# A softmax-like loop partly on GpSimd, two earlier weight streams and a finer side job in an eight-core transformer kernel

## The reference

```python
xn = _layernorm(x, axis=-1)
# attention-like branch
qkv = _rms(xn) @ w_qkv.T
q, k, v = jnp.split(qkv, 3, axis=-1)
q = _rms(q); k = _rms(k)
w = jnp.exp(k)
kv_cum = jnp.cumsum(w * v, axis=1)
w_cum = jnp.cumsum(w, axis=1)
y = jax.nn.sigmoid(q) * (kv_cum / (w_cum + 1e-06))
u, g = jnp.split(y @ w_swiglu.T, 2, axis=-1)          # 2 x 8192
attn = xn + u * jax.nn.silu(g) @ w_out.T
# second branch, fwht: Walsh-Hadamard transform of the last axis
t = fwht(xn * SU_ug) / SCALE
t = silu(t @ W_gate.T * (Wscale_ug[INTER:] * SCALE)) * (t @ W_up.T * (Wscale_ug[:INTER] * SCALE))
ffn = (fwht(t * SU_dp) / SCALE) @ W_down.T * (Wscale_dp * SCALE)
return x + attn + ffn
```

## Time and profile before

| | us |
|---|---|
| Three runs: median | 12506.38 |
| Three runs: lowest, highest | 11569.87, 12691.81 |
| The profiled execution, its own time | 11569.87 |
| Its span, slowest core | 11568.3 |
| Busy, TensorE matmul | 8165.5 (71%) |
| Busy, VectorE | 4189.6 (36%) |
| Busy, ScalarE | 1977.1 (17%) |
| Busy, GpSimd (DMA issues, all but four small memsets) | 437.3 (4%) |

### The profile page before, as it was taken

The page is one execution under the profiler, slowest core; times in us unless marked ns, Lnnn a source line. Parts: engine busy times, 40 slices in busy tenths (PEclk is TensorE's granted clock), DMA queues, the critical chain, the costliest instruction groups (busy, mean ns, idle before and its releaser), DMA issues. The chain is left out here.

```text
span 11568.3 us, 100573 instructions; the slowest of 8 cores (11511.4 to 11568.3 us)
## 1 busy us (share of the span) xinstructions
PE 8165.5 (71%) x35072; PEld 3480.9 (30%) x35072; DVE 4189.6 (36%) x4832; ACT 1977.1 (17%) x2180; POOL 437.3 (4%) x796
## 2 busy tenths in 40 slices
PE   3555552895225466377787788888888869797979
PEld 1222220342002122133333333333333324343434
DVE  4445551565650361377677751111111110000111
ACT  1111111000011231211111111222222223230000
POOL 0000000000000000000000000000000000000000
PEclk8777776997568788699899999999999979898989
DMA  4111101211110011233433332222222235554343
GB/s 73 44 44 44 44 30 65 96 73 29 22 38 33 33 45 59 70 122 109 137 117 116 132 110 79 96 81 75 81 74 81 75 118 171 179 172 155 130 160 119
DMA packets 289699, 1021.78 MB, mean 88 GB/s; under 512 B 32691, under 2 KB 147379, under 8 KB 241587
## 3 DMA queue, kind: packets, MB, share of 16 engines
q1 hardware_dynamic: 209270, 772.00, 19.7%
q0 software_dynamic: 79936, 243.34, 7.8%
HBM read 855.81 MB, written 201.35 MB: 91 GB/s over the span
## 5 line engine op out<-in xcount | busy, mean ns | idle before, releaser
L108 PE MATMUL ps_u<-A_big,wt 128*128 128x512 bf16 x8192 | 2011.3, 402 | 886.0 <-ACT wt L108 760.3
L108 PE MATMUL ps_o<-A_big,wt 128*128 128x512 bf16 x8192 | 1776.9, 380 | 298.8 <-ACT wt L108 163.6
L108 PE MATMUL ps_g<-A_big,wt 128*128 128x512 bf16 x8192 | 1851.7, 379 | 0.0
L108 PE MATMUL ps_m<-A_big 128*128 128x512 bf16 x6144 | 1357.3, 385 | 274.1 <-DMA kslabA<-wf_sp 227.5
L108 PEld LDWEIGHTS ps_u<-A_big,wt 128*128 128x128 bf16 x8192 | 829.5, 102 | 2007.8 <-issue 1164.6
L108 PEld LDWEIGHTS ps_o<-A_big,wt 128*128 128x128 bf16 x8192 | 803.2, 98 | 1274.6 <-issue 313.6
L108 PEld LDWEIGHTS ps_g<-A_big,wt 128*128 128x128 bf16 x8192 | 801.2, 98 | 966.9
L108 PE MATMUL ps_m<-A_big,wt 128*128 128x512 bf16 x3072 | 790.4, 419 | 350.8 <-ACT wt L108 279.6
L108 PEld LDWEIGHTS ps_m<-A_big 128*128 128x128 bf16 x6144 | 606.8, 99 | 1037.8 <-issue 332.7
L108 DVE TENSOR_TENSOR midb<-usb,sgf 128x512 bf16<-128x512 bf16 x512 | 354.4, 692 | 1455.7 <-ACT sgf L108 1403.7
L108 ACT CAST wt<-ldb 128x2048 bf16<-128x2048 f32 (+1 forms) x352 | 586.2, 1665 | 459.0 <-DMA ldb<-wswT 236.3
(11 more groups left out here) (110 smaller groups left out, 4681.2 us busy)
## 6 DMA issues: line engine op xcount, KB each, us to landing
ldb<-wswT SPq DMA_DIRECT2D x128, 1024.0 KB, 6.2
ldb<-wugT SPq DMA_DIRECT2D x128, 1024.0 KB, 5.7
wdb<-wdownT SPq DMA_DIRECT2D x16, 4096.0 KB
ldbA<-woutT SPq DMA_DIRECT2D x128, 512.0 KB, 4.4
ldbB<-woutT SPq DMA_DIRECT2D x128, 512.0 KB, 4.7
wt<-wdh_sp SPq DMA_DIRECT2D x32, 2048.0 KB, 10.1
ldb<-wqkvT SPq DMA_DIRECT2D x96, 512.0 KB, 4.6
psw_sp<-midb POOLq DMA_DIRECT2D x256, 128.0 KB, 2.0
```

The source lines that it names most:

```text
L108: r = getattr(h, meth)(*args, **kw)
```

## The change

Four edits. First, in the exp loop of foreign K the multiply into `wtmp` is issued on GpSimd; the sum stays on VectorE, with `redc` of two columns used in turn; the masked accumulate becomes a multiply into `redt` and an add into `carryW`, both on GpSimd. GpSimd's instructions get a semaphore of their own (PO) and, like those of VectorE and ScalarE, a wait for all earlier ones of their engine. The store of `kslab` waits for ScalarE alone. Second, the first two V blocks are streamed before `sig_rows` and the own exp loop, not after. Third, the first two Q blocks are streamed before the last two `v_chain`s. Fourth, `what_gen` yields after each single instruction, and `next(side_gen)` is called three times a tile: once between `usb` and `midb`, twice after `midb`.

```diff
--- before.py
+++ after.py
@@ -48,10 +48,10 @@
     def __init__(self, nc):
         self.nc = nc
         self.sems = {}
         self.streams = None
 
-    AUTO = {"vector": "DV", "scalar": "AC"}
+    AUTO = {"vector": "DV", "scalar": "AC", "gpsimd": "PO"}
 
     def q(self, eng, meth, *args, w=(), i=None, **kw):
         if eng in self.AUTO and meth not in ("_wait_only_", "dma_start"):
...
@@ -334,7 +334,8 @@
             bcs = S("bcs", [128, 2 * TTK], F32)
             t1f = S("t1f", [128, TTK], F32)
             wtmp = S("wtmp", [128, TTK], F32)
-            redc = S("redc", [128, 1], F32)
+            redt = S("redt", [128, 2], F32)
+            redc = S("redc", [128, 2], F32)
             ps_m = (P("ps_m0", [128, TTK], F32), P("ps_m1", [128, TTK], F32))
             ps_s = (P("ps_s0", [1, TTK], F32), P("ps_s1", [1, TTK], F32))
             ps_sq = (P("ps_sq0", [1, TTK], F32), P("ps_sq1", [1, TTK], F32))
@@ -429,9 +430,10 @@
                     xc = xbf[:, c * TTK:(c + 1) * TTK]
                     wv = []
                     if c == 0:
+                        wv = [("PO", kb.cnt["PO"])]
                         if it >= 2:
-                            wv = [("PE", bigpe[it - 2]),
-                                  (f"SX{par}", xqsp[it - 2])]
+                            wv += [("PE", bigpe[it - 2]),
+                                   (f"SX{par}", xqsp[it - 2])]
                     kb.q("vector", "tensor_mul", t1f[:, :], xc, bcs[:, 0:TTK])
                     dv = kb.q("vector", "tensor_sub",
                               xqf[:, c * TTK:(c + 1) * TTK], t1f[:, :],
@@ -505,23 +507,30 @@
                 sigbcdv[prev] = kb.q("vector", "tensor_copy", t1f[:, :],
                                      ps_b1[:, :], w=[("PE", pe)], i=("DV", 1))
                 ac_p = None
+                po_mac = {}
                 dv = None
                 for j in range(KCH):
                     ks = kslab[:, j * TTK:(j + 1) * TTK]
+                    rj = redc[:, j % 2:j % 2 + 1]
                     wv = [("AC", ac_p)] if ac_p else []
-                    kb.q("vector", "tensor_mul", wtmp[:, :], ks, t1f[:, :],
-                         w=wv)
-                    d2 = kb.q("vector", "engine_nop", i=("DV", 1))
+                    wv.append(("DV", sigbcdv[prev]))
+                    po = kb.q("gpsimd", "tensor_mul", wtmp[:, :], ks,
+                              t1f[:, :], w=wv)
                     ac_p = kb.q("scalar", "activation", ks, wtmp[:, :], AF.Exp,
-                                w=[("DV", d2)], i=("AC", 1))
-                    kb.q("vector", "reduce_sum", redc[:, :], ks, axis=AX.X,
-                         w=[("AC", ac_p)])
-                    dv = kb.q("vector", "scalar_tensor_tensor",
-                              carryW[:, j:j + 1], redc[:, :],
-                              cmsk[:, f3:f3 + 1], carryW[:, j:j + 1],
-                              ALU.mult, ALU.add, i=("DV", 1))
+                                w=[("PO", po)], i=("AC", 1))
+                    wv2 = [("AC", ac_p)]
+                    if j >= 2:
+                        wv2.append(("PO", po_mac[j - 2]))
+                    dv = kb.q("vector", "reduce_sum", rj, ks, axis=AX.X,
+                              w=wv2, i=("DV", 1))
+                    tj = redt[:, j % 2:j % 2 + 1]
+                    kb.q("gpsimd", "tensor_mul", tj, rj,
+                         cmsk[:, f3:f3 + 1], w=[("DV", dv)])
+                    po_mac[j] = kb.q("gpsimd", "tensor_add",
+                                     carryW[:, j:j + 1], carryW[:, j:j + 1],
+                                     tj)
                 wsp[prev] = kb.dma("gpsimd", wf_sp[f3, tt, :, :], kslab[:, :],
-                                   sem="SPI", w=[("DV", dv), ("AC", ac_p)])
+                                   sem="SPI", w=[("AC", ac_p)])
                 bigpe[prev] = kb.cnt["PE"]
 
             emit_cast(0)
@@ -801,6 +810,9 @@
                 evac[pp] = [("DV", d1), ("AC", a2)]
             mmdone[par] = kb.cnt["PE"]
         kb.q("vector", "_wait_only_", w=[("PE", kb.cnt["PE"])])
+        vpar = {}
+        vpar[0] = stream_oc(32 + 0, 0)
+        vpar[1] = stream_oc(32 + 1, 1)
         for tt in range(NT):
             sig_rows(ps_st[tt], tt, bca[:, 0:T], ps_b1)
         ac_p = None
@@ -811,10 +823,6 @@
             ac_p = kb.q("scalar", "activation", kwr_row(j), scf[:, 0:T], AF.Exp,
                         w=[("DV", dv)], i=("AC", 1))
             wexp_ac[j] = ac_p
-
-        vpar = {}
-        vpar[0] = stream_oc(32 + 0, 0)
-        vpar[1] = stream_oc(32 + 1, 1)
 
         def v_chain(j):
             kb.q("vector", "tensor_mul", wvt[:, :], kwr_row(j),
@@ -847,14 +855,17 @@
             mmdone[par] = kb.cnt["PE"]
             if j + 2 < KCH:
                 vpar[j + 2] = stream_oc(32 + j + 2, j + 2)
+            if j == KCH - 1:
+                qpar0 = stream_oc(0, 0)
+                qpar1 = stream_oc(1, 1)
             if j >= 1:
                 v_chain(j - 1)
         dv = v_chain(KCH - 1)
 
         qsp = {}
         qpar = {}
-        qpar[0] = stream_oc(0, 0)
-        qpar[1] = stream_oc(1, 1)
+        qpar[0] = qpar0
+        qpar[1] = qpar1
         for j in range(KCH):
             par = qpar[j]
             for tt in range(NT):
@@ -1037,6 +1048,8 @@
                         ev_u[pp] = kb.q("vector", "tensor_copy", usb[:, S0:S1],
                                         ps_u[pp][:, :], w=[("PE", pe_u)],
                                         i=("DV", 1))
+                    if side_gen is not None:
+                        next(side_gen, None)
                     key = (p, tt)
                     wv = [("AC", ev_g[pp]), ("DV", ev_u[pp])]
                     if key in spq:
@@ -1106,7 +1120,9 @@
                             "p (b w) -> p b w", w=width)
                         kb.q("vector", "tensor_sub", sp_v, a_v, b_v, w=wv)
                         wv = ()
+                        yield
                         kb.q("vector", "tensor_add", a_v, a_v, b_v)
+                        yield
                         dv = kb.q("vector", "tensor_copy", b_v, sp_v,
                                   i=("DV", 1))
                         yield
```

More of the change, by code:

```diff
@@ L50, in __init__ @@
         self.sems = {}
-        self.cnt = {n: 0 for n in ("PH", "LD", "LW0", "LW1", "LQ", "LP0", "LP1", "SPI", "SQ0", "SQ1", "SM0", "SM1", "SO0", "SO1", "LC", "LC1", "SX0", "SX1", "LQ1", "PE", "DV", "AC")}
+        self.cnt = {n: 0 for n in ("PH", "LD", "LW0", "LW1", "LQ", "LP0", "LP1", "SPI", "SQ0", "SQ1", "SM0", "SM1", "SO0", "SO1", "LC", "LC1", "SX0", "SX1", "LQ1", "PO", "PE", "DV", "AC")}
         self.streams = None
-    AUTO = {"vector": "DV", "scalar": "AC"}
+    AUTO = {"vector": "DV", "scalar": "AC", "gpsimd": "PO"}
     def q(self, eng, meth, *args, w=(), i=None, **kw):
@@ L172, in _build @@
     for sname in ("PH", "LD", "LW0", "LW1", "LQ", "LP0", "LP1", "SPI", "SQ0",
-                  "SQ1", "SM0", "SM1", "SO0", "SO1", "LC", "LC1", "SX0", "SX1", "LQ1",
+                  "SQ1", "SM0", "SM1", "SO0", "SO1", "LC", "LC1", "SX0", "SX1", "LQ1", "PO",
                   "PE", "DV", "AC"):
```

## The result

| us | before | after |
|---|---|---|
| Median of 14 executions | 12107.06 | 12451.89 |
| Lowest to highest | 11561.34 to 12717.74 | 11786.43 to 12888.67 |
| The lowest two | 11561.34, 11563.09 | 11786.43, 11789.38 |

Compared like with like, the ratio after to before is 1.0193, with a 95% interval of 1.0163 to 1.0223: slower by 1.9%, at the edge of the 2% that counts as a difference here. The lowest times differ by 225 us. The forecast was 11826, or +256 us on an execution of 11570. The median of all fourteen, 12451.89, lies outside the range of 11620 to 12060.

What follows compares the result with a forecast made beforehand. No engine was taken as full throughout: foreign K was a chain of waits, the pair phase bound by VectorE, then TensorE after the side job. Sum: 11570 + 191 - 4 + 69 = 11826 us, range 11620 to 12060.

Steps and rivals of the forecast that it cites:

- the forecast one: Whole kernel: GpSimd chain in foreign K plus ten tiles behind the side job, 11826 us; chance 0.60.
- forecast +191: Foreign K's exp loop: a 3.93 us step through GpSimd, ScalarE and VectorE, +15.9 us a loop, twelve times.
- X: GpSimd's 128x512 multiply in foreign K's exp loop: taken as 1.2 us, bounds 0.69 to 1.38, far above 3.34.
- h: Hop from VectorE's sum to GpSimd's small multiply in the exp loop: taken as 0.4 us, high end 0.61.
- steps that overlap: Rival, exp loop: GpSimd begins the next multiply during the sum; step 2.20 us, -120 us, kernel 11515 us; chance 0.04.
- forecast -4: V's and Q's weights streamed earlier: about 2 us gained by each; together between a loss and a gain of 12.
- slip of the Ln: ScalarE's Ln of the last-but-one V chain starts about 7 us later, behind Q's casts and loads.
- forecast +69: Side job in single steps, pair phase: +77 us for ten tiles less 8 for shorter idle; high end +96.
- lost slot: Side job: chunks of 12.33 tiles, not 13; last copy at tile 197, not 207; ten tiles after it, +77 us.
- the -8: VectorE under the side job: 186.7 pairs of usb and midb at 1.59 us less 176 at 1.73.
- check of a chunk: Side job before: 12 x 6.12 + 11 x 1.73 + 29.15 = 121.6 us, matching sixteen loads 121.6 apart.
- relieves TensorE: Rival, pair phase: TensorE's 81.6 us of waits for usb go and no tile is lost; -82, 11675 us; chance 0.08.

Runs made afterwards that it cites:

- e5: Edit 1 on the kernel before, with GpSimd's next multiply issued ahead of the two small instructions and wtmp in two halves: foreign K 165.6 us earlier, span 164 us shorter.
- e6: Kernel before, nothing on GpSimd, VectorE's next multiply issued ahead of the sum, wtmp in two halves: foreign K 174.6 us earlier, cores on average 164 us less.
- e3: Edits 2 and 3 alone on the kernel before: 11503.8 to 11570.2 us over eight cores, a mean of 3 us less on die 0.
- e2: Edit 4 alone on the kernel before: pair phase 2340.9 us, lowest time 11627.43 us, +57.7 us.
- e2b: Edit 4 alone on the kernel before, run again for a profile: pair phase 2336.9 us against 2282.8.
- e4: Edit 4 on the kernel before, with two more empty calls behind each store (39 calls, 13 tiles a chunk): pair phase 29.6 us shorter, span 25.
- e1: Edit 1 alone on the kernel before: foreign K 159.5 us longer, lowest time 11737.62 us against 11569.76.
- e10: Kernel before with the next pair's weight loads issued ahead of this pair's tiles: pair phase 17 us shorter, span 6.5.
- e12: Kernel before with VectorE's multiply one chunk ahead, the side job in three parts and weight loads first: lowest 11155.35 us against 11561.88, a factor of 0.965.

## Why the prediction came out as it did

**The case was right, the median was not.** Of the cases, the forecast one happened: a chain through GpSimd, and ten tiles behind the side job. What failed is the base of the sum, 11570, with the sentence "so the forecast is for an execution like it". The range was laid round the lowest of three executions, which was 7.5% under their median, while fourteen executions of the same kernel before spread from 11561.34 to 12717.74. The range took in the price of every edit and left out this larger spread of the metric itself. On the basis it was made for, the error is 31 us (+225 against +256); on the median it is 626. The median of the three, 12506.38, would have given 12762, again 311 off: three executions don't fix a median here.

**Edit 1, forecast +191, measured +157.** 157 / 12 is 13.1 us a loop, not 15.9. The step is 3.73 us, not 3.93 (a row with two engines is a hop, from the end of the one's instruction to the start of the other's):

| term, us | forecast | after |
|---|---|---|
| multiply X | 1.2 | 1.16 |
| GpSimd to ScalarE | 0.2 | 0.15 |
| exp | 0.63 | 0.63 |
| ScalarE to VectorE | 0.17 | 0.23 |
| sum | 0.69 | 0.69 |
| h, VectorE to GpSimd | 0.4 | 0.20 |
| two small instructions | 0.44 | 0.38 |
| their two gaps | 0.20 | 0.29 |

X was well placed, a little under 1.2. The Trainium skill (GPSIMD Engine Reference, 3.1 Elementwise) had led to an estimate of 1.12; the measured 1157 ns lies between it and the value taken. The term that was mis-sized is h. It was put half-way between a hop of 0.17 and a store's delay of 0.61 us behind VectorE, and an arithmetic instruction starts three times sooner than the store, 0.20 us. At fifteen steps and twelve loops 0.2 us make 36 us, as much as the whole error of 34; the other terms cancel.

The cause given was the queue's order, and e5 and e6 show it. The rival "steps that overlap" had been put at a step of 2.20 us and 36.3 us a loop, which the order of the queue ruled out; once e5 changes that order the step is 1.97 and the gain 166 us, more than the 120 it was given. The prediction saw that multiply j+1 stood behind a wait for sum j, but priced it only as a loss against before. It did not ask whether before had the same fault. It had: VectorE's queue, too, held multiply j+1 behind sum j, at 2.89 us a step, where e6 needs 1.91 for the same instructions without the nop.

**Edits 2 and 3, forecast -4, measured about -3 (e3).** Too small to be told from nothing. The slip of the Ln, put at about 7 us, is 8.6 (4445.33 to 4453.95), and V is as long as before. Q is 7.5 us longer in after, and 2 us in e3. Of the 7.5, 3.1 us lie between the last `qtmp` and the first `psw_sp` store (169.4 us against 166.3), where e2, e2b and e4 have 170.0 to 170.5: that is edit 4, whose first side step stands in front of the first `midb`. The other 4.4 us can't be told from the differences between cores: from the first to the last `qtmp` the cores 0 to 3 take 428.7 to 438.1 us in after, but 426.6 to 440.4 in e1, which has none of edits 2 to 4.

**Edit 4, forecast +69, measured +50 (die 0; +54 to +58 in e2b and e2).** The lost slot is right: the last copy falls on tile 197 and not 207, and on core 2 78.4 us more lie behind the side job (381.2 to 459.6), forecast 77. The gap in front of `midb` shrank to 0.10, as written. The term that was mis-sized is the -8: the side job itself became 20 us shorter on core 2 (1929.7 to 1909.7, from its first load to its last store). In before, every fourth chunk takes 102.7 to 104.4 us on core 2 from its first subtract to its last copy, the others 92.3 to 92.7, since VectorE waits in it for TensorE (5.1 us before `usb` and 3.7 before `midb` in the fourth). In after only two of the sixteen are so long, 104.3 and 103.1. In e10, whose weights are loaded earlier, none is (92.3 to 93.1 on core 1), so the long ones come from weights that are late. The prediction had no such term. Its check of a chunk, 121.6 us, came out by luck: the gap of 29.15 us that it read the earlier trace rows is the longest of the fifteen on that core, whose mean is 26.7, and the longer chunks made up the difference. The spacing of the loads on core 2 went from (6716.0 - 4903.9) / 15 = 120.8 to (6865.0 - 5060.7) / 15 = 120.3. The rival "relieves TensorE" is partly true, since e4 gains 25 to 30 us without losing the slot; it was given 82.

**What the prediction left unasked.** It named the gap's load and the 441.2 us of waits for weights behind it, and took both as fixed. 129.8 of the 441.2 are the phase's first wait, ahead of any side job, and e12 has it too (128.3 on core 1). The others and the waits for `usb` were the largest thing in the phase, 256 us, but behind two locks, of which neither alone gives more than 40.

## What to carry to other kernels

Where in-order engines pass work to one another, look first at what stands in front of the next step in each queue, and move that; here, moving the work to a free engine added a hop and left the wait where it was (+157 us, against -166 with the same engines in another order). An empty slot in a hand-paced side job may be the cover of a stall or the place of the last tiles: count the slots before and after. When the removal of one wait gives little, read the waits again for what took its place before giving the idea up: here two locks on the same work paid only together (40 and 17 us alone, 249 both). And where executions of one kernel spread more than the change is worth, say which execution a forecast is for, or give its range the spread.

## What was not expected of the hardware

A 128x1 operation on GpSimd took 0.19 us with VectorE idle or at a one-input sum, but 0.37 to 0.40 in nearly all cases beside a VectorE operation with two inputs. The timeline of core 5 of e5, at the end of a loop:

```profile
674.31 0.97 DVE L108 TENSOR_TENSOR sqbf<-xbfB 128x512 bf16<-128x512 bf16 x2
674.41 0.37 POOL L108 TENSOR_TENSOR redt<-redc,cmsk 128x1 f32<-128x1 f32 x1 [1.24 <-DVE redc L108]
...
674.93 0.40 POOL L108 TENSOR_TENSOR carryW<-carryW,redt 128x1 f32<-128x1 f32 x1
```

The Trainium skill (SBUF — State Buffer, Who interferes with whom) has one port pair shared by the two engines, which a two-input VectorE operation can hold against GpSimd; these rows agree with it: the small instructions end at 674.79 and 675.33, the two products that the first row puts together at 674.74 and 675.28. In this change it costs nothing, because GpSimd's multiply runs with VectorE idle, and in e5 beside the one-input sum (1158 ns against 1151 without it).

GpSimd's store of `midb` took 620 ns on average to issue in after where it took 542 in before. It is the side job's copy alone that does it. Core 2 of after:

```profile
5325.59 1.23 DVE L108 COPY wdb<-wspare 128x2048 f32<-128x2048 f32 x1
...
5326.02 0.91 POOL L108 DMA_DIRECT2D psw_sp<-midb  x1 [32.28 <-DVE midb L108]
```

The 54 issues that fell beside such a copy took 899 to 1264 ns, the other 202 took 539 to 556, whether VectorE was idle or at the side job's subtract or add; in before none fell beside a copy. The store waits for `midb` anyway and has 2255.8 us of idle time in front of it in all.
